# Turning patches as a rounded part and a remainder, straight out of the convolution

## The reference

```
red  = mean of the window's 9 patches
q    = layernorm(red) @ la_wq                       # 8 heads of 32
k, v = layernorm(patch) @ la_wkv                    # for each of the 9 patches
attn = softmax over the 9 patches of (q * 256**-0.5) . k
local = red + (attn . v) @ la_proj_w + la_proj_b
gk, gv = layernorm(local) @ ga_wkv                  # for a class token over the 9 windows
token = local @ mod_w + mod_b
```

## Time and profile before

| | us |
|---|---|
| median of 3 runs | 796.1 (794.16 to 797.16) |
| the profiled execution: its time, its span | 795.92, 794.1 |
| token stage: the convolutions end at | 305 |
| busy in the span: PE, DVE, ACT, POOL | 710.0, 508.0, 378.9, 425.8 |
| mean granted TensorE clock | 0.941 |

### The profile page before, as it was taken

How to read it: one execution, slowest core, us unless ns; L and a number is a source line. 1 busy time by engine, 2 the same in 40 slices (tenths; PEclk the granted TensorE clock), 3 DMA queues, 4 the chain that set the end, 5 groups by cost and what they waited for, 6 DMA issues and landing times.

```text
span 794.1 us, 13086 instructions
## 1 busy us (share of the span) xinstructions
PE 710.0 (89%) x4247; PEld 607.2 (76%) x4247; DVE 508.0 (64%) x1228; ACT 378.9 (48%) x932; POOL 425.8 (54%) x360
## 2 busy tenths in 40 slices
PE   3999999999999999999828819999999999587898
PEld 3889998898989887554627718999999999344786
DVE  3688877877877777768989861332233223478957
ACT  4586665766666655433132413444444444066131
POOL 5777867768587761549769421433443332136640
PEclk9999999999999999999858958999999999689799
DMA  7955233332343030000020088999989881300001
GB/s 236 260 147 154 76 114 100 116 115 60 115 116 113 4 107 1 1 0 1 0 107 0 27 323 299 309 323 327 340 315 327 332 331 60 139 2 2 0 1 67
DMA packets 47084, 108.58 MB, mean 137 GB/s; under 512 B 5048, under 2 KB 24748, under 8 KB 39596
## 3 DMA queue, kind: packets, MB, share of 16 engines
q1 hardware_dynamic: 44428, 100.68, 37.9%
q0 software_dynamic: 2592, 7.10, 2.5%
HBM read 101.58 MB, written 6.17 MB: 136 GB/s over the span
## 4 chain that ended last, share of the span: by engine, by line
PE 76%; DVE 13%; DMA 3%; ACT 2%; POOL 2%; issue 2%; SPq 1%; DVEq 0%; ACTq 0%; POOLq 0%
PE banks L1728 12%; PE banks L1736 12%; PE banks L291 9%; PE banks L293 9%; PE banks L292 9%; PE banks L298 6%; PE banks L304 4%; PE banks L1336 3%; PE banks L1383 2%; DVE banks L1510 1%; PE banks L1310 1%; DVE a_o L1601 1%; DVE a_prod L1223 1%; PE banks L1366 1%; DMA xraw<-in_x_rest 1%
## 5 line engine op out<-in xcount | busy, mean ns | idle before, releaser
L417 POOL TENSOR_TENSOR x_lo<-xraw,x_hi 128x512 fp32r<-128x512 f32 x81 | 106.1, 1310 | 77.6 <-ACT x_hi L411 77.5
L1819 ACT ACTIVATE hid<-banks,b 128x128 f32<-128x128 f32 x216 | 79.3, 367 | 110.3 <-PE banks L1728 110.3
L291 PE MATMUL banks<-wc_hi,x_hi 128*128 128x256 f32 x324 | 97.9, 302 | 12.7 <-POOL x_hi L420 10.0
L293 PE MATMUL banks<-wc_hi,x_lo 128*128 128x256 f32 x324 | 93.0, 287 | 0.0
L292 PE MATMUL banks<-wc_lo,x_hi 128*128 128x256 f32 x324 | 92.8, 286 | 0.0
L1984 DVE TENSOR_TENSOR res<-banks,xb 128x256 f32<-128x256 f32 x27 | 11.5, 424 | 127.0 <-PE banks L1736 127.0
L1857 POOL TENSOR_TENSOR y<-bve,mhalf 128x1 f32<-128x1 f32 x27 | 20.4, 755 | 104.8 <-DVE bve L1992 104.8
L453 DVE BATCH_NORM_STATS2 stats<-banks 128x6 f32<-128x256 f32 x81 | 34.6, 427 | 62.8 <-ACT pe_sb L447 62.1
L291 PEld LDWEIGHTS banks<-wc_hi,x_hi 128*128 128x128 f32 x324 | 63.0, 194 | 14.8 <-issue 10.2
L1728 PEld LDWEIGHTS banks<-xT,w_raw 128*128 128x128 f32 x448 | 67.9, 196 | 5.8 <-ACT xT L1807 0.9
L291 PE MATMUL banks<-wkv_hi,xg_hi 128*128 128x512 f32 x162 | 70.4, 435 | 0.5 <-DVE prod L545 0.3
(11 more groups left out here) (334 smaller groups left out, 1856.2 us busy)
## 6 DMA issues: line engine op xcount, KB each, us to landing
w_raw<-in_w SPq DMA_DIRECT2D x28, 1024.0 KB, 6.7
xraw<-in_x_main SPq DMA_DIRECT2D x26, 768.0 KB
w1more<-in_w SPq DMA_DIRECT2D x13, 1024.0 KB, 5.9
w2more<-in_w SPq DMA_DIRECT2D x13, 1024.0 KB, 8.4
xraw<-in_x_rest SPq DMA_DIRECT2D x48, 96.0 KB
xraw<-in_x_rest SPq DMA_DIRECT2D x26, 114.0 KB
yl<-y_rows SPq DMA_DIRECT2D x2, 1028.0 KB, 6.9
a_w<-in_qkv_w SPq DMA_DIRECT2D x2, 768.0 KB, 5.3
```

The costliest lines, as they stand in the source:

```text
L291: pe.matmul(dst, a[0], b[0], start=start, stop=False)
L293: return pe.matmul(dst, a[1], b[0], start=False, stop=stop)
L417: pool.tensor_tensor(x_lo[:, i % RING_X, :], xraw[:, k, 0:KF].rearrange("p c b -> p (c b)"), x_hi[:, i % RING_X, 0:KF * P], ALU.subtract). ...
L1819: act.activation(hid[:, s % 2, fc, :], bank(fc % 2, 0, P), ACT.Gelu, bias=b1[:, bass.ds(e * FC + fc, 1)]).then_inc(sem("gelu_made"), 1)
```

## The change

The normalization moves behind the turn. A layernorm is (x - mean) * rstd; the mean is taken out by la_wkv itself: the mean of its scaled rows is subtracted from each row, once, in the lead-in (agg holds the gain / 256, and a second product with la_wkv gives that mean in bank 5). The factor rstd is applied where keys and values are read: copy_v scales by it, and key_product becomes a scalar_tensor_tensor with it. What is turned is then the raw convolution, split on its way out of the bank: copy_pe writes pe_hi in rounded form, and measure gains a subtraction that writes pe_lo. Both are turned by a rounded product with a rounded identity, ident_r: four matmuls of 128x128 in place of two transposes, into one bank of 512 columns. One ScalarE copy of 512 columns, copy_xg, takes the place of split_xT_hi and split_xT_lo. Since hi and lo parts have few mantissa bits, the product with the identity hands them on as they are.

A convolution now waits for pe_lo_made in place of summed. rstd is computed once for all 10 rows of a window, in rstd_w with two slots, at its end. The rings change to make room: RING_X from 8 to 7, local from 9 windows to 4. ScalarE makes ident_r at its start, and PE waits for that. The renaming of the experts' xg to xrows has no effect.

```diff
-RING_X = 8
-RING_XN = 4
+RING_LOCAL = 4
+RING_X = 7
         def conv(pe, i):
             if i >= 2:
-                pe.wait_ge(sem("summed"), i - 1)
+                pe.wait_ge(sem("pe_lo_made"), i - 1)
...
         def copy_pe(act, i):
             if i >= RING_PE:
-                act.wait_ge(sem("xn_made"), i - RING_PE + 1)
+                act.wait_ge(sem("xT_done"), i - RING_PE + 1)
             act.wait_ge(sem("conv_done"), i + 1)
-            act.activation(pe_sb[:, i % RING_PE, :], bank(i % 2), ACT.Copy).then_inc(sem("pe_copied"), 1)
+            act.activation(pe_hi[:, i % RING_PE, :], bank(i % 2), ACT.Copy).then_inc(sem("pe_copied"), 1)
...
                 dve.tensor_tensor(total, bank(i % 2), total, ALU.add).then_inc(sem("summed"), 1)
+            dve.tensor_tensor(pe_lo[:, i % RING_PE, :], bank(i % 2), pe_hi[:, i % RING_PE, :], ALU.subtract)\
+               .then_inc(sem("pe_lo_made"), 1)
...
+        def window_std(pool, n):
             if n > 0:
-                pool.wait_ge(sem("xn_made"), NP * (n - 1) + EARLY_KEYS)
-            inverse_std(pool, window_batch(n, 0), 0, EARLY_KEYS)
...
+            if n > 1:
+                pool.wait_ge(sem("key_used"), NP * (n - 1))
+            pool.wait_ge(sem("var_made"), window_batch(n) + 1)
+            pool.tensor_tensor(rstd_w[:, n % 2, :], veps[0][:, :], mhalf[:, :], ALU.pow).then_inc(sem("rstd_made"), 1)
...
-        def normalize_patch(act, j):
...
-            normalize(act, patch_rows(j), pe_sb[:, j % RING_PE, :], k).then_inc(sem("xn_made"), 1)
         def turn_patch(pe, j):
-            pe.wait_ge(sem("xn_made"), j + 1)
+            pe.wait_ge(sem("pe_lo_made"), j + 1)
             if j >= 2:
-                pe.wait_ge(sem("xg_lo_made"), j - 1)
-            turn(pe, bank(2 + j % 2), patch_rows(j)).then_inc(sem("xT_done"), 1)
+                pe.wait_ge(sem("xg_made"), j - 1)
+            for i, part_of in enumerate((pe_hi, pe_lo)):
+                for c in range(CH):
+                    last = pe.matmul(bank(2 + j % 2, i * C + c * P, i * C + (c + 1) * P),
+                                     part_of[:, j % RING_PE, c * P:(c + 1) * P], ident_r[:, :], start=True, stop=True)
+            last.then_inc(sem("xT_done"), 1)
-        def split_xT_hi(act, j):
+        def copy_xg(act, j):
             if j >= 2:
                 act.wait_ge(sem("kv_done"), j - 1)
             act.wait_ge(sem("xT_done"), j + 1)
-            act.activation(xg_hi[:, j % 2, :], bank(2 + j % 2), ACT.Copy).then_inc(sem("xg_hi_made"), 1)
-        def split_xT_lo(dve, j):
-            dve.wait_ge(sem("xg_hi_made"), j + 1)
-            dve.tensor_tensor(xg_lo[:, j % 2, :], bank(2 + j % 2), xg_hi[:, j % 2, :], ALU.subtract)\
-               .then_inc(sem("xg_lo_made"), 1)
+            act.activation(xg[:, j % 2, :, :].rearrange("p i c -> p (i c)"), bank(2 + j % 2, 0, 2 * C), ACT.Copy)\
+               .then_inc(sem("xg_made"), 1)
         def project_kv(pe, j):
-            pe.wait_ge(sem("xg_lo_made"), j + 1)
+            pe.wait_ge(sem("xg_made"), j + 1)
...
-            act.activation(v_sb[:, n % 2, k, :], bank(4 + j % 2, C, 2 * C), ACT.Copy).then_inc(sem("kv_copied"), 1)
+            act.activation(v_sb[:, n % 2, k, :], bank(4 + j % 2, C, 2 * C), ACT.Identity, scale=rstd_w[:, n % 2, k:k + 1])\
+               .then_inc(sem("kv_copied"), 1)
...
-            dve.tensor_tensor(prod[:, k * C:(k + 1) * C], bank(4 + j % 2), q_sb[:, :], ALU.mult).then_inc(sem("key_used"), 1)
+            dve.scalar_tensor_tensor(out=prod[:, k * C:(k + 1) * C], in0=bank(4 + j % 2), scalar=rstd_w[:, n % 2, k:k + 1],
+                                     in1=q_sb[:, :], op0=ALU.mult, op1=ALU.mult).then_inc(sem("key_used"), 1)
...
                 if i == 2:
-                    pe.wait_ge(sem("wkv_prepared"), CH)
-                    mm_rows(pe, bank(4, 0, 2 * C), aggT, wkv_raw, 0, 2 * C).then_inc(sem("kvb_done"), 1)
+                    pe.wait_ge(sem("wkv_prepared"), 2 * CH)
+                    mm_rows(pe, bank(4, 0, 2 * C), aggT, wkv_raw, 0, 2 * C)
+                    mm_rows(pe, bank(5, 0, 2 * C), agg, wkv_raw, 0, 2 * C).then_inc(sem("kvb_done"), 1)
...
-                dve.tensor_scalar(wkv_raw[:, c, :], wkv_raw[:, c, :], vecs[:, LAKV + c:LAKV + c + 1], None, ALU.mult)\
-                   .then_inc(sem("wkv_prepared"), 1)
+                dve.scalar_tensor_tensor(out=wkv_raw[:, c, :], in0=wkv_raw[:, c, :], scalar=vecs[:, LAKV + c:LAKV + c + 1],
+                                         in1=bank(5, 0, 2 * C), op0=ALU.mult, op1=ALU.subtract).then_inc(sem("wkv_prepared"), 1)
```

More of the change, by code:

```diff
@@ L117, in vision_tower @@
         x_lo = sb("x_lo", [P, RING_X, KF * P], F32R, tok)
-        pe_sb = sb("pe_sb", [P, RING_PE, C], F32, tok)
+        pe_hi = sb("pe_hi", [P, RING_PE, C], F32R, tok)
+        pe_lo = sb("pe_lo", [P, RING_PE, C], F32R, tok)
         gv_sb = sb("gv_sb", [P, NP, C], F32, tok)
-        xg_hi = sb("xg_hi", [P, 2, C], F32R, tok)
-        xg_lo = sb("xg_lo", [P, 2, C], F32R, tok)
+        xg = sb("xg", [P, 2, 2, C], F32R, tok)
         v_sb = sb("v_sb", [P, 2, NP, C], F32, tok)
@@ L147, in vision_tower, with local_at @@
         w_gkv = gv_sb[:, NP - 3 * CH:NP - CH, :].rearrange("p (c k) n -> p c (k n)", c=CH)
-        tail_raw = local[:, (NW - 1) * C:NW * C]
-        tail_hi, tail_lo = xg_lo[:, 0, :], xg_lo[:, 1, :]
+        tail_raw = local[:, (RING_LOCAL - 1) * C:RING_LOCAL * C]
+        def local_at(n):
+            return local[:, n % RING_LOCAL * C:(n % RING_LOCAL + 1) * C]
+        tail_hi, tail_lo = xg[:, 1, 0, :], xg[:, 1, 1, :]
         w_gproj = sb("w_gproj", [P, CH, C], F32, tok)
@@ L152, in vision_tower @@
         rows = sb("rows", [P, len(ROWS) * C], F32, tok)
-        localT = sb("localT", [P, 2, C], F32, tok)
+        localT = wkv_raw[:, 0, :].rearrange("p (i c) -> p i c", i=2)
         a_bias = vprod[0:64, 0:QKV]
@@ L326, in vision_tower, with window_batch @@
                    ("low rank", 0, T - BT), ("low rank", T - BT, T)]
-        CLASS_ROW = 2
-        def window_batch(n, late):
-            return 2 * n + late + (n > 0)
+        CLASS_ROW = 1
+        def window_batch(n):
+            return n + (n > 0)
         def batch_of(which, part):
             n = [i for i, b in enumerate(BATCHES) if b[0] == which][part]
-            return (2 * NW + 1 + n,) + BATCHES[n][1:] + (SET[which],)
+            return (NW + 1 + n,) + BATCHES[n][1:] + (SET[which],)
         def inverse_std(pool, n, a=0, b=T, i=0):
@@ new lines, in window_std, with red_shift @@
+            if n > 1:
+                pool.wait_ge(sem("key_used"), NP * (n - 1))
+            pool.wait_ge(sem("var_made"), window_batch(n) + 1)
+            pool.tensor_tensor(rstd_w[:, n % 2, :], veps[0][:, :], mhalf[:, :], ALU.pow).then_inc(sem("rstd_made"), 1)
+        def red_shift(dve, n):
+            dve.wait_ge(sem("rstd_made"), window_batch(n) + 1)
+            dve.scalar_tensor_tensor(out=nmr[0][:, NP:T], in0=mv[0][:, NP:T, 0], scalar=-1.0, in1=rstd_w[:, n % 2, NP:T],
+                                     op0=ALU.mult, op1=ALU.mult).then_inc(sem("nmr_made"), 1)
@@ L527, in project_kv @@
             for c in range(CH):
-                a = [x[:, j % 2, c * P:(c + 1) * P] for x in (xg_hi, xg_lo)]
+                a = [xg[:, j % 2, i, c * P:(c + 1) * P] for i in range(2)]
                 last = mm3(pe, dst, a, (wkv_hi[:, c, :], wkv_lo[:, c, :]), c == 0, c == CH - 1)
@@ L552, in normalize_red @@
         def normalize_red(act, n):
-            act.wait_ge(sem("nmr_made"), window_batch(n, 1) + 1)
+            act.wait_ge(sem("nmr_made"), window_batch(n) + 1)
             if n > 0:
                 act.wait_ge(sem("redT_done"), n)
-            normalize(act, redn[:, :], red_sum[:, n % 2, :], NP).then_inc(sem("redn_made"), 1)
+            act.activation(redn[:, :], red_sum[:, n % 2, :], ACT.Identity, scale=rstd_w[:, n % 2, NP:T], bias=nmr[0][:, NP:T])\
+               .then_inc(sem("redn_made"), 1)
         def turn_red(pe, n):
@@ L680, in residual @@
             dve.wait_ge(sem("summed"), NP * (n + 1))
-            dve.scalar_tensor_tensor(out=local[:, n * C:(n + 1) * C], in0=red_sum[:, n % 2, :], scalar=1.0 / NP,
+            dve.scalar_tensor_tensor(out=local_at(n), in0=red_sum[:, n % 2, :], scalar=1.0 / NP,
                                      in1=rows[:, 0:C], op0=ALU.mult, op1=ALU.add).then_inc(sem("residual_made"), 1)
@@ L695, in turn_local @@
             pe.wait_ge(sem("redT_made"), CH * min(n + 3, NW))
-            turn(pe, bank(6), local[:, n * C:(n + 1) * C]).then_inc(sem("local_turned"), 1)
+            turn(pe, bank(6), local_at(n)).then_inc(sem("local_turned"), 1)
         def copy_localT(act, n):
@@ L1717, in turn_rows @@
                     pe.wait_ge(sem("tables_made"), 2)
-                turn(pe, bank(6 + s % 2), xg[:, s % AHEAD, :]).then_inc(sem("rows_turned"), 1)
+                turn(pe, bank(6 + s % 2), xrows[:, s % AHEAD, :]).then_inc(sem("rows_turned"), 1)
             def up(s, fc):
@@ L2261, in _ @@
```

(13 more changed lines are left out.)

82 lines of the change are left out of this document (26 added, 56 removed).

## The result

The changed kernel takes 815.75 us (median of 4 runs, 813.66 to 816.91) against 795.99 us before: ratio 1.026, 95% interval 1.0242 to 1.0278. It is slower by 20 us. Run once more in a later comparison it gave 1.0262 (1.0246 to 1.0279).

The account below looks back on a forecast made before the run. The prediction took PE (TensorE) to bound the kernel from 48.7 to 305.0 us. It summed 795.9 + 16.3 (turns) + 3.2 (lead-in) + 0.6 (last window) = 816.0 us, range 805 to 849.

Parts of the forecast that it names:

- The likeliest case: The whole kernel takes 816.0 us, own range 810 to 822, chance 0.56.
- The turn: Transposing a patch on PE: four rounded products at 0.11 us each, 0.44 in place of 0.22 us.
- Rival (a): In the turn, short rounded products run at the unrounded rate, 0.22 us each; total 848.5 us, chance 0.20.
- rival (b): In the turn, loads hide better, 0.06 to 0.085 us a product; total 802 to 809 us, chance 0.14.
- the 8-column records: Token product's four matmuls of 8 columns: 0.085 to 0.11 us each, taken as the weight-load floor.
- How many turns count: Of 81 turns, 74 lie on the path, 67 of them between 48.7 and 305 us: 16.3 us more.
- The lead-in: Before 48.7 us: second bias product, longer scalings, waits for pe_lo and a wider copy add 3.2 us.
- The last window: From 305 to 315 us VectorE's chain stays: remainders gone and added, longer power, wider copy; 0.6 us more.
- Cover: From 48.7 to 305 us PE stays the bound; VectorE's extra work stays under it, and relief elsewhere pays nothing.
- rival (d): Turn as forecast, but VectorE falls behind at each window's end, about 1 us x 8; total 824 us, chance 0.05.
- rival (c): Not slower: PE's waits at the key and value product vanish and the lead-in's product hides; 793 to 797 us, chance 0.05.

Follow-up runs that it names:

- the three edits of the operands: The changed kernel with the turn's moving operand widened to 256 columns, cut to 64, or its stationary operand cut to 64: ratios 1.0264, 1.0244, 1.0083.
- the kernel with the other token product: The kernel before with its token product cut into 256 and 264 columns instead of 512 and 8: 791.88 us, ratio 0.9967.

## Why the prediction was right

The likeliest case came true: 816.0 forecast, 815.75 measured, within its own range of 810 to 822.

Where the time went, by the chains of the two profiles of each kernel (us; the first of a pair is the profile shown):

| | before | changed | growth | forecast |
|---|---|---|---|---|
| to patch 4's turn | 52.19, 52.11 | 56.44, 54.76 | 4.25, 2.65 | 3.2 and two turns, 3.6 |
| to the last convolution's end | 252.82, 252.78 | 267.51, 267.52 | 14.7, 14.7 | 67 turns, 14.7 |
| to the last value copy | 22.68, 22.68 | 24.50, 24.49 | 1.8, 1.8 | 0.6 and five turns, 1.7 |
| the rest of the span | 466.4, 466.2 | 464.4, 466.7 | -2.0, 0.5 | 0 |

**The turn.** Forecast 0.44 us by loads 0.11 apart, measured 0.45. Rival (a), the unrounded rate, would have shown 0.88, and rival (b) 0.25 to 0.34; neither did, and the three edits of the operands show the load as the reason, not only as a fitting number. The reading of the 8-column records, from which the floor was taken, was put to use in the kernel with the other token product and held.

**How many turns count.** Forecast 74, 16.3 us. The 67 of the full stretch are shown, by the second line of the table and by the window's growth of 2.01 us for nine. The seven at the edges are not: the kernel with doubled turns gained 14.8 us with an interval up to 16.2, so the term may be too large by about 1.5 us, or by next to nothing. They were not the turns that the forecast named, either: of the first four it counted patches 0 and 1, and in the changed kernel's chain stand 1, 2 and 3 (44.35, 49.21, 52.72), while patch 0's is made at 40.0 us, when the chain is on VectorE.

**The lead-in.** Up to patch 4's convolution the forecast was 3.0 us and 2.95 were measured (28.69 against 25.74), of which 0.26 is only that the first pixels landed later. The terms: the bias products 4.33 and 3.45 us for eight records (forecast near 4), the scalings 1.31 for two (forecast 1.4), pe_lo 0.34 twice (forecast 0.33). The 4.33 is partly at the lower clock; from 18 to 26 us it was granted at 0.79 in this profile and in both of before, and at 1.00 in the second of the changed kernel, which is most of why that one grew by 2.65 only. From that convolution to patch 4's turn the forecast was 0.64 (the wider copy and two turns), and it is 1.30 in both profiles (27.75 and 27.73 against 26.45 and 26.43). Not foreseen there was the power of 10 elements, for which 2.0 was forecast and 1.97 measured, but at the end of the stage and not here; moving the work behind it gave 0.7 back.

**The last window: right by luck.** Forecast +0.6 and five turns, measured 1.8, so 0.7 for the rest if the five turns cost 1.1. But the path that the forecast counted on is not there. It let VectorE's chain stay, with the power 0.8 longer and remainders added and gone, and the chain of the changed kernel has neither a power nor a remainder in this window. Four loads a turn keep PE the bound for longer: the kernel before with each turn made twice has the same way there, on PE until 325.3 and without a power. The counted path did show in the kernel that moved the norm alone: power 1.98 in place of 1.18, the window 1.3 us longer. That two different paths cost nearly the same is chance.

**Cover.** PE idle in the rounds, rival (d), did not come: 268 us without a gap. Nor did rival (c). The scaled key product takes 0.49 on the chain, within 0.41 to 0.53.

**What came out even by luck.** In the first profile the token stage ends 20.8 us later than before and the rest is 2.0 us shorter; in the second pair the numbers are 19.2 later and 0.5 longer. The forecast's 20.1 lies between, and which side a profile falls on is mostly the clock's doing, on which the forecast said nothing. The rest has nothing of the change in it. Of its 2.0 us 1.7 are the start of the attention, up to its second bias product (331.58 to 336.49 before, 352.47 to 355.67 in the changed kernel), where the clock differed:

```profile
331.00:336.00 5.00, 5.00 (x12) 2.47 (x13) 2.88 (x8) 1.91 (x5) 1.50 (x1) 0.66 0.00 0
```

That is before; at the same work the changed kernel has:

```profile
351.80:356.00 4.20, 4.19 (x15) 2.31 (x15) 3.25 (x9) 2.00 (x5) 0.55 (x1) 1.00 0.00 0
```

## What to carry to other kernels

Where one engine is full, as PE was for 256 us here, count only its instructions; relief elsewhere was worth nothing. On TensorE, count weight loads as well as columns: splitting an operand into two parts before a turn doubles the loads, and does so for a product that is nothing but loads. Splitting behind the turn, on engines that idle, cost nothing here (the window of 33.99 us), and a product with a few columns should ride on one with many (2.6 us here). Before a small gain or loss is read from two profiles, compare the granted clock of the stretch in both.

## What was not expected of the hardware

With loads of 64 weight columns a rounded product of 128 columns took 0.06 us, with loads of 128 it took 0.11. The clock of TensorE differs between runs of one kernel at the same place: in the lead-in from 18 to 26 us it was granted at 0.79 in one profile of the changed kernel and 1.00 in the other, and the eight records of the bias products held 4.33 and 3.45 us. At the start of the attention PE idles 1.41 us in the kernel before and 1.82 in the changed one. Soon after it the clock was at 0.66 of the full clock from 331 to 336 us in the profile of before; in the changed kernel it stayed at 1.00 in the first profile and fell to 0.50 from 352 to 355 us in the second, after the same 1.82 us. Each of the two places is worth 1 to 2 us, so my estimate is that a single profile of this kernel is good to about 2 us.
